# Attention over a ±4-channel window: the edge products of the band read 32 rows instead of 128 and run as a group of their own, in pairs on separate rows of TensorE

## The chip, the cores and the metric

The kernel runs on one NeuronCore of one Trainium2 chip. The metric is the device time of one execution in microseconds (us), the median of the runs shown; lower is better. TensorE (PE in the profile) has a clock of two levels, 1.2 and 2.4 GHz; the profile gives the granted clock as a share of 2.4 GHz, so 0.50 is the lower level.

## What is computed

One block of a MetaFormer on x of 128 images, 256 channels, 9 by 9 pixels (81 pixels, called HW), all in fp32: a layer norm over channels, a convolution-attention part that is added to x, then a mixture of 8 experts (2 for each token) that is added as well. The change sits in the first of the two attentions. Cut to what matters:

```
k1 = grouped 1-d conv of x along channels (9 taps, one kernel per pixel)
a  = softmax over 9 taps of W2 @ relu(bn(W1 @ [x, k1])) + b2     # a[b, d, c]: 9 weights per channel
v  = depthwise 3x3 conv of x + bias                              # v[b, c, h, w]
pad_v = v with 4 channels of zeros on either side
out1[b, c] = sum over d of pad_v[b, c + d] * a[b, d, c]  + k1    # a band of 9 channels around c
out2 = second, spatial attention
x1   = x + alpha * out1 + (1 - alpha) * out2
```

The sum over d is a product with a band matrix: for one image, a 256 by 256 matrix that is zero farther than 4 from its diagonal, times v of 256 channels by 81 pixels.

## The kernel before

The kernel is written engine by engine, with semaphores set by hand; nothing is reordered by a scheduler, so the order on each engine is the order of the code. The stages follow one another: the norm and k1; the two depthwise convolutions; the attention stage; routing of the tokens; the experts; gathering and output.

In the attention stage the images go in 32 groups of 4 (G = 4), and two groups make one turn of the loop (PAIRS = 16). For each group, PE does these steps, named as in the code:

- keys (line 514): the logits' first layer, 8 matmuls of 512 columns;
- band (lines 565 to 571): the band products of a group one or two steps older;
- spatial_1, tap_logits and spatial_2 (lines 524 and 526, 541, 533): the second attention's layers and the tap logits;
- unmasked (line 553): transposes that turn expanded tap weights into the band matrices of a group.

pe_turn writes the order out by hand: keys, band (odd group of the turn before), spatial_1, tap_logits, spatial_2, unmasked, then the same for the second group of the pair with the even group's band.

band splits the 256 channels in two halves of 128 rows, since PE takes 128 input rows and 128 output rows at a time. Four products are needed for an image. Two are full: output channels 0 to 127 from input channels 0 to 127 (a0_s, columns 0 to 127, into bank 6 of the accumulator ps), and output channels 128 to 255 from input channels 128 to 255 (a1_s, columns 32 to 159, into bank 7). Two are edges: the last output channels of the first half also need the first channels of the second half (a1_s, columns 0 to 31, into rows 96 to 127 of bank 6), and the first 4 output channels of the second half need the last channels of the first (a0_s, columns 128 to 131, into rows 0 to 3 of bank 7). Outside the band a0_s and a1_s hold zeros. Four images lie side by side in each bank, 81 columns each. `start=True` on a matmul makes it overwrite, `start=False` makes it add to what is there.

Around band: DVE makes a0_s and a1_s in mask_bands (lines 891 and 893, semaphore msk_c) and adds the result to x1 in add_band (line 918, which waits for band_p). GpSimd (POOL) waits for band_p too, before it loads v of a later group into vc_s (line 1463). SyncE (SP) loads the other inputs of a group when DVE has finished the group two before it. ACT does the activations. One fp32 matmul of the code shows in the trace as two pieces on PE, each with a weight load of its own (PEld).

Of the kernel before, what the change touches and what calls it, by code (L numbers as in the profile page):

```python
# [5 lines left out]
HW = H * W  # L6
# [7 lines left out]
G = 4  # L14
# [33 lines left out]
def metaformer_kernel(nc, x, taps, tap_bn, tap_rows, toeplitz_mask, ident, band_masks, rot_masks, zstrings,  # L48
# [14 lines left out]
    with ctx:  # L63
# [46 lines left out]
        def take(parts, *dims):  # L110
            n = 1
            for d in dims:
                n *= d
            a = pool_[0:parts, cursor[0]:cursor[0] + n]
            cursor[0] += n
            assert cursor[0] <= C * HW
            names = "abcde"[:len(dims)]
            if len(dims) > 1:
                a = a.rearrange(f"p ({' '.join(names)}) -> p {' '.join(names)}",
                                **{m: d for m, d in zip(names, dims)})  # L120
            return a
# [26 lines left out]
        ps = ctx.enter_context(nc.psum_tensor("ps", [128, 8, 512], fp32))  # L148
# [24 lines left out]
        xc_s, vc_s, kc_s, xr_s, kr_s = (take(128, 2, HALVES, G, HW) for _ in range(5))  # L173
# [7 lines left out]
        a0_s = take(128, G, BAND0)  # L181
        a1_s = take(128, G, BAND1)
# [236 lines left out]
        def _(pe):  # L419
# [48 lines left out]
            with pe.Fori(0, C // CHUNK) as i:  # L468
# [4 lines left out]
                for n in range(9):  # L473
# [4 lines left out]
                    for m in range(9):  # L478
                        last = nc.tensor.matmul(flat[:, m * 2 * CHUNK:(m + 1) * 2 * CHUNK].rearrange("p (v c) -> p v c", v=2),
                                                mask_s[:, n * 9 + m, :],  # L480
                                                tapc_s[:, :, :],
                                                start=True, stop=True)
                    last.then_inc(S["mb_p"], 1)
                for k in range(per_chunk):
                    q, par = i * per_chunk + k, k % 2
# [9 lines left out]
                    for c in range(QUAD):  # L495
                        o = ps[:, b0 + c // 2, (c % 2) * 2 * HW:(c % 2 + 1) * 2 * HW]
                        last = nc.tensor.matmul(o, pt_s[:, par, c, :], m_s[:, k * QUAD + c, :, :]  # L497
                                                .rearrange("p v n -> p (v n)"), start=True, stop=True)
# [4 lines left out]
            for h in range(HALVES):  # L503
                last = nc.tensor.matmul(ps[:, 6, 0:EXPERTS], ones_s[:, :], router_s[:, h, :], start=h == 0, stop=h == 1)
# [52 lines left out]
            def band(g, par, i):  # L557

                pe.wait_ge(S[f"v_in{par}"], 32 * i)
                pe.wait_ge(S["msk_c"], 2 * (g + 1) + CREDIT)  # L560
                pe.wait_ge(S["x1_c"], g + CREDIT)
                for b in range(G):
                    v0, v1 = vc_s[:, par, 0, b, :], vc_s[:, par, 1, b, :]
                    o = slice(b * HW, (b + 1) * HW)
                    nc.tensor.matmul(ps[:, 6, o], a0_s[:, b, 0:128], v0, start=True, stop=False,  # L565
                                     skip_group_check=True)
                    nc.tensor.matmul(ps[96:128, 6, o], a1_s[:, b, 0:32], v1, start=False, stop=True,  # L567
                                     skip_group_check=True)
                    nc.tensor.matmul(ps[:, 7, o], a1_s[:, b, 32:160], v1, start=True, stop=False,  # L569
                                     skip_group_check=True)  # L570
                    last = nc.tensor.matmul(ps[0:4, 7, o], a0_s[:, b, 128:132], v0, start=False, stop=True,  # L571
                                            skip_group_check=True)
                last.then_inc(S["band_p"], 1)

            def pe_turn(i, first=False, front=True, back=True, late=True):

                if front:
                    keys(2 * i, 0, i, first)
                if late:
                    band(2 * i - 3, 1, i - 1)  # L580
                if front:
                    spatial_1(2 * i, 0, i)
                    tap_logits(2 * i, 0)
                    spatial_2(2 * i)
                if back:
                    unmasked(2 * i - 2, 0, i)
                if front:
                    keys(2 * i + 1, 1, i)
                if back:
                    band(2 * i - 2, 0, i)  # L590
                if front:
                    spatial_1(2 * i + 1, 1, i)
                    tap_logits(2 * i + 1, 1)
                    spatial_2(2 * i + 1)
                if back:
                    unmasked(2 * i - 1, 1, i)
# [4 lines left out]
            with pe.Fori(2, PAIRS) as i:  # L601
                pe_turn(i)
            pe_turn(PAIRS, front=False)
            band(GROUPS - 1, 1, PAIRS)

# [985 lines left out]
```

## Time and profile before

| | |
|---|---|
| device time, median of 3 runs | 1827.84 us (1827.51 to 1829.89) |
| span of the one profiled execution | 1881.2 us (no other time is recorded for it) |
| PE busy, share of the span | 76% |
| DVE, ACT, POOL busy | 60%, 40%, 34% |
| attention stage in the profiled execution | about 384 to 875 us |

A share of the whole span is an average over stages with different limits; the rows further down are of the attention stage alone. PE's records are pipelined: two matmuls that follow each other overlap in their durations, so what one costs is read from the distance between the ends of two, as the chain view gives it. That chain is followed back from the last instruction: at each step to what released it, or to the instruction before it on its engine.

### The profile page before, as it was taken

The page shows a single profiled execution, that of the slowest core. Times are in us where ns is not written, and L with a number is a line of the kernel's source. Part 1 is how long each engine was busy: PE and PEld are TensorE (multiplying, and loading weights), DVE is VectorE, ACT ScalarE, POOL GpSimd, SP SyncE. Part 2 cuts the span into 40 slices and gives each one's busy share as a digit, 9 for nine tenths or more (in the row PEclk, how much of TensorE's full clock was granted, in tenths as well). Part 3 has the DMA queues.
Part 4 walks back from the last instruction along what each step waited for, and adds up shares of the span by engine and source line. Part 5 has one row for each costly group of instructions (what it writes and reads, how often), then busy time and mean ns, then how long its engine had stood idle before and what let it go on. Part 6 is the DMA issues. An engine that isn't in the chain of part 4 may idle for free.

```text
span 1881.2 us, 38992 instructions
## 1 busy us (share of the span) xinstructions
PE 1423.0 (76%) x9926; PEld 1155.6 (61%) x9927; DVE 1127.2 (60%) x3074; ACT 753.2 (40%) x1752; POOL 648.2 (34%) x561
## 2 busy tenths in 40 slices
PE   0485889879999999998454442899999999993222
PEld 0474888846666666666444442688888888882111
DVE  6893333346766766764677667466666666663333
ACT  0572444434444434433565553333333333332211
POOL 0350111123333334330555555255555455441000
PEclk9996788789999999995555555899999999996555
DMA  8434454377667667641333234223332333324999
GB/s 291 114 107 167 167 191 179 146 205 187 153 151 182 152 157 172 154 112 55 104 98 110 93 104 142 77 84 90 90 90 86 92 93 90 90 74 129 194 197 159
DMA packets 310870, 250.50 MB, mean 133 GB/s; under 512 B 184329, under 2 KB 289374, under 8 KB 310132
## 3 DMA queue, kind: packets, MB, share of 16 engines
q1 hardware_dynamic: 290527, 196.96, 40.4%
q0 software_dynamic: 20320, 53.28, 8.6%
q8 instruction: 9, 0.15, 0.0%
q14 instruction: 14, 0.11, 0.0%
HBM read 152.07 MB, written 105.57 MB: 137 GB/s over the span
## 4 chain that ended last, share of the span: by engine, by line
PE 65%; DVE 12%; DMA 8%; issue 6%; ACT 4%; SPq 3%; another core or an unknown queue 1%; DVEq 1%; ACTq 0%; POOLq 0%; POOL 0%
PE ps L690 13%; PE ps L675 12%; PE ps L514 6%; DMA aux<-y_d 4%; PE ps L497 4%; PE ps L463 4%; PE ps L541 3%; PE ps L569 3%; PE ps L565 2%; ACT pool_ L1267 2%; PE ps L524 2%; PE ps L659 2%; PE ps L533 2%; PE ps L567 2%; PE ps L526 2%
## 5 line engine op out<-in xcount | busy, mean ns | idle before, releaser
L1491 POOL DMA_INDIRECT y_d<-pool_,to_s x176 | 254.9, 1449 | 285.6 <-DVE pool_ L1184 249.4
L690 PE MATMUL ps<-pool_,aux 128*128 x2112 | 249.8, 274 | 5.2 <-DVE aux L1176 3.5
L675 PE MATMUL ps<-aux,pool_ 128*128 128x256 f16 x2112 | 247.4, 274 | 0.8 <-ACT aux L1391 0.6
L690 PEld LDWEIGHTS ps<-pool_,aux 128*128 128x128 f16 x2112 | 198.5, 98 | 50.8 <-issue 23.7
L675 PEld LDWEIGHTS ps<-aux,pool_ 128*128 x2112 | 207.0, 98 | 25.9 <-issue 1.4
L1471 POOL DMA_INDIRECT rows_d<-aux,idx_s x162 | 157.9, 975 | 159.3 <-issue 87.3
L1391 ACT ACTIVATE aux<-ps,b_s 128x256 f32<-128x256 f32 x352 | 138.4, 475 | 162.5 <-DVE aux L1176 162.1
L1184 DVE SCALAR_TENSOR_TENSOR pool_<-ps,pool_ 128x512 f32<-128x512 f32 x88 | 60.9, 692 | 140.2 <-PE ps L690 140.2
L1463 POOL DMA_DIRECT2D pool_<-v_d x64 | 50.1, 783 | 271.1 <-PE ps L571 269.8
L718 PE MATMUL ps<-ident_s,aux 128*128 128x128 f32 x162 | 41.6, 429 | 122.4 <-DVE aux L1216 122.4
L514 PE MATMUL ps<-pool_,se_w_s 81*81 81x512 f32 x256 | 118.7, 607 | 6.0 <-DMA pool_<-k_d 6.0
L1383 ACT ACTIVATE aux<-ps 128x512 f16<-128x512 f32 x88 | 52.5, 597 | 174.9 <-PE ps L659 174.9
L718 PEld LDWEIGHTS ps<-ident_s,aux 128*128 128x128 f32 x162 | 30.8, 221 | 133.0 <-DVE aux L1216 133.0
L1176 DVE TENSOR_TENSOR aux<-aux 128x1024 f16<-128x1024 f32 x88 | 107.8, 1225 | 3.1
L1302 ACT ACTIVATE pool_<-ps,sa_ab 128x324 f32<-128x324 f32 x64 | 39.7, 621 | 160.0 <-PE ps L526 160.0
L1447 POOL COPY aux<-big 128x324 f32 x64 | 29.3, 459 | 213.9 <-PE ps L463 184.7
L1216 DVE SCALAR_TENSOR_TENSOR aux<-aux,wt_s 128x256 f32<-128x256 f32 x81 | 34.5, 481 | 105.4 <-ACT aux L1409 103.6
L463 PE MATMUL ps<-ident_s,aux 128*81 128x128 f32 x512 | 76.8, 299 | 25.5 <-POOL aux L1447 25.5
L853 DVE COPY aux<-ps 81x512 f32<-81x512 f32 x64 | 43.9, 686 | 86.0 <-PE ps L463 86.0
L632 PE MATMUL ps<-aux,before_s 128*128 128x8 f32 x54 | 16.0, 370 | 103.9 <-DVE aux L1059 80.8
L1314 ACT ACTIVATE pool_<-ps,pool_ 128x81 f32<-128x81 f32 x256 | 79.7, 338 | 29.1 <-DVE pool_ L884 29.1
L497 PE MATMUL ps<-pool_,aux 82*128 82x162 f32 x512 | 90.0, 325 | 0.0
(203 smaller groups left out, 3160.9 us busy)
## 6 DMA issues: line engine op xcount, KB each, us to landing
pool_<-rows_d SPq DMA_DIRECT2D x88, 258.0 KB
aux<-y_d SPq DMA_DIRECT2D x54, 384.0 KB, 7.1
big<-in_x SPq DMA_DIRECT2D x2, 5184.0 KB, 21.0
xn_d<-big SPq DMA_DIRECT2D x16, 648.0 KB, 3.0
v_d<-aux SPq DMA_DIRECT2D x64, 162.0 KB, 2.0
ks_d<-aux SPq DMA_DIRECT2D x64, 162.0 KB, 2.0
pool_<-xn_d SPq DMA_DIRECT2D x32, 324.0 KB
pool_<-k_d SPq DMA_DIRECT2D x32, 324.0 KB
```

The costliest lines, as they stand in the source:

```text
L463: last = nc.tensor.matmul(ps[0:HW, 4 + par, c * BS:(c + 1) * BS], xq_s[:, par, c, :], ident_s[:, :], start=True, stop=True)
L497: last = nc.tensor.matmul(o, pt_s[:, par, c, :], m_s[:, k * QUAD + c, :, :] .rearrange("p v n -> p (v n)"), start=True, stop=True)
L514: last = nc.tensor.matmul(ps[0:HW, n, :], se_w1_s[:, k, :], kq_s[:, par, k, 2 * n:2 * n + 2, :].rearrange("p b j -> p (b j)"), start=k == ...
L675: last = nc.tensor.matmul(o, w_s[:, a, bass.ds(e * (4 * PIECE) + (k * HID + j * 128), 128)], xh_s[:, par, b, k * SLOTS:(k + 1) * SLOTS], s ...
L690: last = nc.tensor.matmul(ps[:, 6 + par, s * C:(s + 1) * C], hh_s[:, par, a, j, s * 128:(s + 1) * 128], w_s[:, b, bass.ds(e * (4 * PIECE) ...
L718: last = nc.tensor.transpose(ps[:, 2 * par + h, s * 128:(s + 1) * 128], mix_s[:, par, s, h * 128:(h + 1) * 128], ident_s[:, :])
L1176: nc.vector.tensor_tensor(lo, hf_s, hi, ALU.subtract).then_inc(S["hlo_c"], 1)
L1184: nc.vector.scalar_tensor_tensor(yo_s[:, par], ps[:, 6 + par, :].rearrange("p (s c) -> p s c", s=2), 1.0 / WSCALE, b2_s[:, bass.ds(e * C, ...
L1314: ins = nc.scalar.activation(e_s[:, par, h, b, :], ps[:, 2 + h, b * HW:(b + 1) * HW], ACT.Exp, bias=sm_s[:, par, 2, j:j + 1], accum_out=sm ...
L1391: nc.scalar.activation(hf_s[:, j * SLOTS:(j + 1) * SLOTS], ps[:, 2 + 2 * par + j // 2, (j % 2) * SLOTS:(j % 2 + 1) * SLOTS], ACT.Gelu, bia ...
L1471: nc.gpsimd.indirect_dma_start(out=rows_d[:, :], out_offset=bass.IndirectOffsetOnAxis(ap=idx_s[:, slot, k:k + 1], axis=0), in_=xf_s[:, slo ...
L1491: nc.gpsimd.indirect_dma_start(out=y_d[:, :], out_offset=bass.IndirectOffsetOnAxis(ap=to_s[:, par, k:k + 1], axis=0), in_=yo_s[:, par, k, ...
```

## The change

The full products of a group's four images come first, the edges after them in a loop of their own. An edge now names only the 32 input rows in which its band matrix is not zero: rows 0 to 31 of the second half for the one, rows 96 to 127 of the first half for the other. The products, their number and their columns are the same. Since all images of a group lie in one bank, only the first full product into each bank now has `start` set. The last edge signals band_p as before. No wait is added or removed.

```diff
                 for b in range(G):
                     v0, v1 = vc_s[:, par, 0, b, :], vc_s[:, par, 1, b, :]
                     o = slice(b * HW, (b + 1) * HW)
-                    nc.tensor.matmul(ps[:, 6, o], a0_s[:, b, 0:128], v0, start=True, stop=False,
+                    nc.tensor.matmul(ps[:, 6, o], a0_s[:, b, 0:128], v0, start=b == 0, stop=False,
                                      skip_group_check=True)
-                    nc.tensor.matmul(ps[96:128, 6, o], a1_s[:, b, 0:32], v1, start=False, stop=True,
+                    nc.tensor.matmul(ps[:, 7, o], a1_s[:, b, 32:160], v1, start=b == 0, stop=False,
                                      skip_group_check=True)
-                    nc.tensor.matmul(ps[:, 7, o], a1_s[:, b, 32:160], v1, start=True, stop=False,
+                for b in range(G):
+                    v0, v1 = vc_s[96:128, par, 0, b, :], vc_s[0:32, par, 1, b, :]
+                    o = slice(b * HW, (b + 1) * HW)
+                    nc.tensor.matmul(ps[96:128, 6, o], a1_s[0:32, b, 0:32], v1, start=False, stop=True,
                                      skip_group_check=True)
-                    last = nc.tensor.matmul(ps[0:4, 7, o], a0_s[:, b, 128:132], v0, start=False, stop=True,
+                    last = nc.tensor.matmul(ps[0:4, 7, o], a0_s[96:128, b, 128:132], v0, start=False, stop=True,
                                             skip_group_check=True)
                 last.then_inc(S["band_p"], 1)
```

Only PE's order changes, and only inside band. The first place is in the loop over the turns, where PE comes from keys (line 514) into band; a row is a line of the code, the operation, what it writes and reads, and the output's rows by columns. Before:

```order
L514 MATMUL ps<-pool_,se_w_s 81x512 x4
L559 ISA
L560 ISA
L561 REGISTER_ALU
L565 MATMUL ps<-pool_ 128x81
L567 MATMUL ps<-pool_ 32x81
L569 MATMUL ps<-pool_ 128x81
L571 MATMUL ps<-pool_ 4x81
```

The same place in the changed kernel, where line 565 is still the full product into bank 6 and line 567 is now the full product into bank 7:

```order
L514 MATMUL ps<-pool_,se_w_s 81x512 x4
L559 ISA
L560 ISA
L561 REGISTER_ALU
L565 MATMUL ps<-pool_ 128x81
L567 MATMUL ps<-pool_ 128x81
L565 MATMUL ps<-pool_ 128x81
L567 MATMUL ps<-pool_ 128x81
```

Each image had full, edge, full, edge; now the eight full products of a group stand together.

The second place is the end of the same band, before spatial_1 (line 524). Before:

```order
L569 MATMUL ps<-pool_ 128x81
L571 MATMUL ps<-pool_ 4x81
L521 REGISTER_ALU
L522 REGISTER_ALU
L524 MATMUL ps<-pool_,sa_w_s 128x324
```

After, with the edges at lines 572 (32 output rows) and 574 (4 output rows):

```order
L567 MATMUL ps<-pool_ 128x81
L572 MATMUL ps<-pool_ 32x81
L574 MATMUL ps<-pool_ 4x81
L572 MATMUL ps<-pool_ 32x81
L574 MATMUL ps<-pool_ 4x81
L572 MATMUL ps<-pool_ 32x81
L574 MATMUL ps<-pool_ 4x81
L572 MATMUL ps<-pool_ 32x81
L574 MATMUL ps<-pool_ 4x81
L521 REGISTER_ALU
L522 REGISTER_ALU
L524 MATMUL ps<-pool_,sa_w_s 128x324
```

The eight edges of the group now follow its last full product, the two kinds in turn.

## Rows read from the trace of the kernel before

**Rows 1.** The page: granted clock in 40 slices; the chain by engine.

```profile
PEclk9996788789999999995555555899999999996555
...
PE 65%; DVE 12%; DMA 8%; issue 6%; ACT 4%; SPq 3%; another core or an unknown queue 1%; DVEq 1%; ACTq 0%; POOLq 0%; POOL 0%
```

**Rows 2.** Stretches: start:end, us, busy by engine, granted clock, DMA share, GB/s.

```profile
427.20:835.00 407.80, 407.80 (x2164) 267.46 (x2163) 279.37 (x636) 173.72 (x592) 142.80 (x112) 1.00 0.67 161
840.00:854.30 14.30, 9.28 (x45) 6.01 (x43) 13.41 (x33) 4.71 (x18) 2.58 (x3) 0.69 0.10 23
854.34:862.65 8.31, 8.31 (x33) 5.15 (x34) 0.00 (x0) 0.00 (x0) 0.00 (x0) 0.50 0.00 1
```

**Rows 3.** The chain through one group: start us, us, engine, line, pieces.

```profile
639.35 3.43 PE ps L514 x8
642.78 0.18 PE ps L565 x2
642.97 0.26 PE ps L567 x2
643.23 0.38 PE ps L569 x2
643.61 0.23 PE ps L571 x2
643.84 0.38 PE ps L565 x2
...
647.59 0.74 PE ps L524 x2
648.33 0.55 PE ps L526 x2
...
652.84 0.87 PE ps L553 x8
653.72 3.44 PE ps L514 x8
```

**Rows 4.** Weight loads by shape, 452.58 to 826.12 us: busy us, mean ns, idle before.

```profile
L565 PEld LDWEIGHTS ps<-pool_ 128*128 128x128 f32 x208 | 33.1, 188 | 24.6 <-issue 13.4
...
L567 PEld LDWEIGHTS ps<-pool_ 128*32 128x32 f32 x208 | 14.3, 108 | 8.5
L571 PEld LDWEIGHTS ps<-pool_ 128*4 128x4 f32 x208 | 9.4, 84 | 8.5
```

**Rows 5.** The chain through the second last group's band and the transposes behind it.

```profile
854.34 0.69 PE ps L565 x2
855.03 0.41 PE ps L567 x2
855.44 0.65 PE ps L569 x2
856.09 0.36 PE ps L571 x2
...
862.65 1.90 PE ps L553 x8
```

**Rows 6.** DVE in order of time, one turn: start, us, instruction, idle before, releaser.

```profile
637.97 1.04 DVE L874 TENSOR_REDUCE pool_<-ps 128x4 f32<-128x324 f32 x2 [3.77 <-PE ps L533]
...
650.25 0.82 DVE L918 TENSOR_TENSOR big<-big,ps 128x648 f32 x1
652.34 1.04 DVE L874 TENSOR_REDUCE pool_<-ps 128x4 f32<-128x324 f32 x2 [1.27 <-PE ps L533]
...
655.11 0.48 DVE L893 TENSOR_TENSOR pool_<-ps,band_s 128x320 f32<-128x320 f32 x1
...
662.10 0.83 DVE L918 TENSOR_TENSOR big<-big,ps 128x648 f32 x1 [1.61 <-PE ps L571]
666.70 1.04 DVE L874 TENSOR_REDUCE pool_<-ps 128x4 f32<-128x324 f32 x2 [3.77 <-PE ps L533]
```

**Rows 7.** The chain's last long wait for a load in the attention stage.

```profile
416.77 6.81 DMA pool_<-k_d
```

## The prediction, made before the changed kernel ran

> **What bounds the kernel now.** I began with the page's row of the granted clock and its chain by engine: PE holds most of the chain, and the clock is at its upper level from the tenth slice to the eighteenth [rows 1]. A share of the whole span says nothing about band, so I cut out the stretch from the first band to the last one that runs at full pace. From 427.20 to 835.00 us PE is busy for all of 407.80 us, at a granted clock of 1.00 (2.4 GHz), while DVE is busy for 69% of it and the DMA engines for 67% [rows 2]. So PE's own stream of instructions is the limit there, and what it no longer has to do shortens the stage, as long as nobody else becomes the limit.
>
> Next I followed the chain through one group. It goes through PE's steps one after another without a wait; keys begin at 639.35 and again at 653.72, so a group costs 14.37 us [rows 3]. 28 such periods and one band (28 x 14.37 + 4.8 = 407 us) fill the stretch, which makes 29 bands in it. Of the other three, one runs beside DVE's chain after 840 us, and the last two run at 1.2 GHz: in the stretch of the second last one the granted clock is 0.50 [rows 2].
>
> **What a band costs, taken apart.** A band takes from 642.78 to 647.59 us, 4.81 us [rows 3]. Its first product shows 0.18 us, later full ones 0.38, the 32-row edge 0.26, the 4-row edge 0.23; 0.18 + 0.26 + 0.38 + 0.23 + 3 x (0.38 + 0.26 + 0.38 + 0.23) = 4.80.
>
> The streaming of columns: keys take 3.43 us for 8 pieces of 512 columns, 0.84 ns a column, so a piece of 81 columns streams for 0.068 us, and the two pieces of a product for 0.136. The weight loads: 128 columns show 188 ns, 32 show 108 and 4 show 84 [rows 4]. The 80 ns between the first two go with 96 columns, 0.83 ns each, so the columns take 0.107, 0.027 and 0.003 us.
>
> Now the 4-row edge: 0.23 - 0.136 - 0.003 leaves 0.091. The 32-row edge: 0.26 - 0.136 - 0.027 leaves 0.097. A full product behind an edge: two loads (the second covers the first stream) and one stream are 0.282, and 0.38 - 0.282 leaves 0.098. So about **0.095 us is lost wherever the shape of the product changes**, in which PE neither streams nor loads. Two rows bear it out. The first product of the band follows keys without a change of shape and costs 0.18 instead of 0.38. The 8 transposes of one shape cost 0.87 us, 0.109 a piece, which is the load of 128 columns alone: streams and gaps are hidden there [rows 3].
>
> **The change, step by step, at the full clock.**
>
> *The full products.* Sixteen pieces of one shape follow keys: 0.18 us for the first two as now, then 14 x 0.109 = 1.53. Sum 1.71 us.
>
> *Into the edges.* One change of shape, 0.095, and one exposed load, 0.027. Sum 0.12 us.
>
> *The edges.* Eight products, 16 pieces. No row of the trace shows two matmuls on different rows of the array, so I bound this from both sides. If each piece waits for the one before, they take 16 x 0.068 = 1.09 us. If a product runs beside its partner on the other rows, the pieces of one kind still follow each other, and the second kind is one piece behind: 9 x 0.068 = 0.61 us. A third, worse end: every step from one kind of edge to the other costs what a change of shape costs now; then the edges keep today's price, 4 x (0.26 + 0.23) = 1.96 us, and that includes the way in.
>
> The pairing has a rule behind it: the Trainium skill, "TensorE: Matmul & The Clock Gate", section "Part 3: Packing small matmuls — row/col tiling", says that matmuls on different 32-row strips start about 4 ns apart, in program order, while one matmul on 32 rows alone takes as long as on 128. By it the sum is the one with 0.61, and had the edges stayed unpaired, fewer rows would have saved nothing; the trace shows neither. On the third end the skill's "TensorEngine Tiling (Array Packing)", section "Key Properties", says that changing the tiling mode drains the engine and changing only the tile does not. The trace agrees on the first half, with the 0.095 us; by the second half the 1.96 would not come.
>
> *Out of the edges.* The way into spatial_1 is paid in its first product, 0.74 us against 0.55 for the next [rows 3], and stays.
>
> New band: 1.71 + 0.12 + 0.61 = 2.44 us, 2.37 less than 4.81. Over 29 bands: **68.7 us**.
>
> **The last two bands**, at 1.2 GHz. Now (0.69 or 0.65) + 0.41 + 0.65 + 0.36 for an image, 8.31 us for a group [rows 2, 5]. Eight transposes take 1.90 us, so sixteen full pieces 3.80; edges 9 x 0.135 = 1.22, the way in 0.14. Sum 5.16, 3.15 less; **6.3 us** for two. Both lie on the chain, which there runs from DVE's masks through band to add_band.
>
> **Who else must keep up.** A turn of two groups goes from 28.73 to 24.0 us. DVE first: from 637.97 to 651.07 us it works without a wait, 13.1 us, and then waits 1.27 for spatial_2 [rows 6]. With groups of 12.0 us it comes 1.1 us late to the second group of a turn. What is late next: its masks are done at 655.59, and PE comes to that band at about 657.15 (keys at 653.72 plus 3.44 [rows 3]); of these 1.56 us about 0.45 is left. Then it catches up: add_band there waited 1.61 us for band, and 3.77 us pass idle before the next turn [rows 6]. 28.73 less these three waits is 22.1 us, DVE's least for a turn, under 24.0. The DMA engines' 67% of 28.73 us become 80% of 24.0. The v loads of POOL and add_band hang on band_p, which comes earlier. Only at the start do loads end last, before keys at about 423.6 [rows 7]; groups right behind it may catch up with their loads again, and I charge 2 us (between 0 and 4), an estimate from that one wait of 6.81 us and the idle DMA share.
>
> **The sum.** 68.7 + 6.3 - 2 = 73 us. The profiled execution has a span of 1881.2 us, 53.4 over the median of the runs. Where it lost them I can't read; band's distances repeat to 0.01 us, so I carry 73 us over as it is: 1827.8 - 73 = **1755 us**, 4.0% less. Were the stage stretched by the same 2.8%, it would be 2 us less gain. If the way in and out of edges of 32 rows is shorter than today's, 0.04 us in two places of 29 bands give 2 us more. Its own range is 1748 to 1763.
>
> **The rivals.**
>
> *One after another.* The edges of a pair don't overlap: band 2.92 us, 29 x 1.89 = 55, plus 2 x 2.2 at the lower clock, less 1: **1769 us**. For it: the trace never shows two streams at once. Against: nor has it anything that could.
>
> *Every edge pays a change of shape.* Band 1.71 + 1.96 = 3.67, 29 x 1.14 = 33, plus 2.9: **1792 us**. For it: today each step between shapes pays, whichever way. Against: that the two kinds of edges now have the same rows and probably the same size.
>
> *Another engine takes over.* The masks come after PE is ready for band (the 0.45 us above), or a group's loads land late at 80% DMA. Each us of waiting in a turn costs 14 us in all; with one, 1769, with two, 1783. For it: the masks' margin shrinks from 1.56 to 0.45 us and the DMA engines' idle share from 33% to 20%. Against: DVE's 22.1 us.
>
> *The other side: the clock falls.* If TensorE dropped to 1.2 GHz within the stage, a group would take 2 x 9.56 + 5.16 = 24.3 us, 9.9 more than now. It decides from 29 x 2.37 / (9.9 + 2.37) = 5.6 groups on; all 29 would give about **2110 us**. For it: after the idle of 840 to 854 us the clock stays at 0.50 for 8.31 us though PE is busy throughout [rows 2]. Against: in 407.8 us of unbroken work it never fell, and the change leaves fewer gaps (2 for a band, not 16).
>
> *It does nothing.* Only if the unprofiled stage hangs on something the profiled one doesn't, among the 53.4 us: **1828 us**.
>
> **How the numbers follow.** Paired edges 0.52, one after another 0.18, another engine 0.11, every edge pays 0.10: faster 0.91. Nothing 0.03: same. Clock 0.06: slower. 0.2%, or 3.7 us, is about what a measurement of this kernel can tell from no change. The predicted time is that of paired edges. The range goes from 1745 (a few us more than reckoned at the way in and out, no wait at the start) to 1795, which takes in the serial case, the waits and the change of shape at every edge; what it leaves out is the last two cases and some of the edges of the others, under 2 in 10.
>
> **What would show it.** In the chain after, a group of about 12.0 us with: full products at 0.22 us each (0.109 a piece) and no 0.38; the first edge about 0.12 above its stream; edges of a pair in 0.14 us together (paired), 0.27 (one after another) or 0.49 (a change of shape at each). DVE's wait before the second reduction of a turn gone, and PE without a wait at line 565. Granted clock 1.00 throughout. Wrong would be: PE waiting for DVE's masks or for loads in most turns, or a clock below 1.00.

## The result, and the profile after

The changed kernel takes **1765.85 us** (median of 4 runs, 1765.32 to 1772.31) against 1827.67 us for the kernel before beside it (4 runs, 1823.94 to 1829.89): a ratio of 0.9665, 95% interval 0.9642 to 0.9689. The time fell by 61.8 us, where 73 were predicted. One run further down, of the kernel that holds POOL back from the second turn on, fell in a slower state (1867.5 us) and is left out of that kernel's time and ratio. The profiled execution of the changed kernel has a span of 1763.8 us. Behind line 574 its line numbers are 3 higher than before; full products are now lines 565 and 567, edges 572 and 574, DVE's masks 894 and 896.

The page's row of the granted clock, which answers to [rows 1]: the upper level again lasts from the tenth slice to the eighteenth, but a slice is now 44.1 us long, and was 47.0.

```profile
PEclk9995878879999999995555558999999999995555
```

The windows view of the stretch in which bands run at full pace, and of one of two short stretches inside it (columns as in [rows 2]):

```profile
440.00:775.00 335.00, 325.53 (x2037) 229.38 (x2037) 275.12 (x599) 163.17 (x550) 139.35 (x108) 0.99 0.78 184
...
677.40:680.80 3.40, 3.40 (x21) 2.36 (x16) 3.13 (x4) 0.20 (x2) 1.67 (x3) 0.50 0.79 215
```

PE was busy for all of its stretch before [rows 2]. Now it is idle for 9.5 us of 335, at a clock of 0.99, while DVE went from 69% to 82%: DVE is almost the limit too. The second row is one of two dips of the clock to its lower level, 3.4 us each (677.4 and 779.8 us).

The chain through a band that waits for nobody, then one that waits, then the second last one at the lower clock (start, us, what), which answers to [rows 3, 5]:

```profile
621.54 3.44 PE ps L514 x8
624.98 0.18 PE ps L565 x2
625.16 0.22 PE ps L567 x2
...
626.73 0.16 PE ps L572
626.89 0.07 PE ps L574
...
627.40 0.74 PE ps L524 x2
...
649.52 0.41 DVE pool_ L896
649.98 0.45 PE ps L565 x2
...
801.33 0.69 PE ps L565 x2
...
805.01 0.23 PE ps L572
...
806.23 1.90 PE ps L553 x8
```

The first band takes from 624.98 to 627.40, **2.42 us**; 2.44 was predicted, and it was 4.81 [rows 3]. Full products cost 0.22 us instead of 0.38, all eight edges 0.67 us together. The second one comes by way of DVE's mask at line 896, and its first product is dearer by 0.27 us, because its load lies open. The third takes 4.90 us (5.16 predicted, 8.31 before).

PE in order of time, the edges of a group (start, us, line, out<-in, rows*columns, pieces, idle before). Durations overlap; the starts tell:

```profile
649.98 0.45 PE L565 MATMUL ps<-pool_ 128*128 128x81 f32 x2 [1.02 <-DVE pool_ L896]
...
651.92 0.25 PE L572 MATMUL ps<-pool_ 32*32 32x81 f32 x1
651.92 0.30 PE L574 MATMUL ps<-pool_ 32*4 32x81 f32 x2
652.01 0.23 PE L572 MATMUL ps<-pool_ 32*32 32x81 f32 x1
652.07 0.23 PE L574 MATMUL ps<-pool_ 32*4 32x81 f32 x1
```

Each kind starts a piece about every 0.07 us, which is the 0.068 us that 81 columns stream, and both kinds do so at once: the edges run in pairs.

PE's waits from 400 to 800 us (engine, line, releaser: us in total, times, longest):

```profile
PE ps L565 <- DVE pool_ L896: 8.2, 8, 1.0
...
PE ps L514 <- DMA pool_<-k_d: 2.2, 4, 0.7
```

In eight turns PE waits 1.02 us for the masks of the band in the turn's second half, which it never did before. What made DVE late is in its order of time, first two groups that follow each other on DVE, then POOL:

```profile
641.68 1.66 DVE L909 TENSOR_TENSOR pool_<-pool_ 128x648 f32<-128x648 f32 x1
643.38 0.83 DVE L911 TENSOR_TENSOR pool_<-pool_ 128x648 f32<-128x648 f32 x1
644.44 1.88 DVE L913 SCALAR_TENSOR_TENSOR big<-pool_,alpha_s 128x648 f32 x1 [0.23 <-DVE pool_ L911]
...
651.99 0.83 DVE L909 TENSOR_TENSOR pool_<-pool_ 128x648 f32<-128x648 f32 x1
...
653.92 0.89 DVE L913 SCALAR_TENSOR_TENSOR big<-pool_,alpha_s 128x648 f32 x1 [0.23 <-DVE pool_ L911]
...
641.84 1.92 POOL L1459 TENSOR_SCALAR pool_<-pool_,alpha_s 128x648 f32<-128x648 f32 x1
643.95 1.68 POOL L1462 TENSOR_TENSOR pool_<-pool_ 128x648 f32<-128x648 f32 x1 [0.18 <-POOL pool_ L1459]
```

The same two instructions take 1.66 and 1.88 us in the first group and 0.83 and 0.89 in the second. In the first, POOL multiplies and adds (lines 1459, 1462: alpha times k1, plus x) at the same time. That is 1.8 us more on DVE, and of the masks' margin, which the prediction put at 0.45 us, nothing is left. These are the eight turns with a wait. In six others POOL's multiply meets line 911 instead, which then takes 1.32 to 1.71 us (1.46 at 593.74 us, for one), and PE does not wait for the masks.

**The account.** The attention stage went from 384.0–873.8 us to 383.6–814.0, 59.4 us less. Bands gave 29 x 2.39 = 69.3 and the last two 6.8. So 16.7 us went elsewhere, and the rows name 16.0: mask waits 8.2 with 8 x 0.27 of weight loads laid open, 2.2 of waits for keys' inputs, and 2 x 1.7 from the two dips.

### The profile page after: what moved, and what is told of

Its sections match the earlier page's. It is cut to its first block, busy times and chain, and to the rows that moved or that the text cites. A ratio compares the mean times of both kernels' runs of the same rounds, so it can differ in the third digit from the quotient of the medians.

```text
span 1763.8 us, 38992 instructions
## 1 busy us (share of the span) xinstructions
PE 1348.7 (76%) x9926; PEld 1129.9 (64%) x9927; DVE 1137.5 (64%) x3074; ACT 752.9 (43%) x1752; POOL 648.6 (37%) x561
## 4 chain that ended last, share of the span: by engine, by line
PE 53%; DVE 20%; DMA 11%; issue 7%; ACT 4%; SPq 3%; DVEq 1%; ACTq 0%; POOLq 0%; POOL 0%
PE ps L693 14%; PE ps L678 13%; DMA aux<-y_d 5%; PE ps L497 5%; PE ps L463 4%; ACT pool_ L1270 2%; PE ps L514 2%; PE ps L662 2%; DMA pool_<-k_d 2%; PE ps L479 2%; PE ps L541 2%; DVE pool_ L763 1%; PE ps L524 1%; DMA aux<-u_d 1%; PE ps L533 1%
## 5 line engine op out<-in xcount | busy, mean ns | idle before, releaser
L1412 ACT ACTIVATE aux<-aux,wt_s 128x256 f32<-128x256 f32 x81 | 35.2, 497 | 130.3 <-DMA aux<-y_d 130.3
L463 PEld LDWEIGHTS ps<-ident_s,aux 128*81 128x81 f32 x512 | 69.0, 170 | 25.6 <-POOL aux L1450 25.6
## 6 DMA issues: line engine op xcount, KB each, us to landing
aux<-y_d SPq DMA_DIRECT2D x54, 384.0 KB, 6.7
```

Of the source, the lines that this page charges most:

```text
L463: last = nc.tensor.matmul(ps[0:HW, 4 + par, c * BS:(c + 1) * BS], xq_s[:, par, c, :], ident_s[:, :], start=True, stop=True)
```

## The experiments

Two things were to be settled: whether POOL's arithmetic beside DVE is what took the missing 11 us, and what it is about the new edges that saves time: 32 rows, the grouping, or separate rows of PE.

**POOL's arithmetic out of DVE's way.** In the changed kernel, POOL's multiply waits until DVE has finished line 913 of the group before:

```diff
                     pool.wait_ge(S[f"rk_in{par}"], 64 * (i + 1))
+                    pool.wait_ge(S["t_c"], g + CREDIT)
                     settle()
```

> The changed kernel, and POOL starts its multiply and add for a group (lines 1459 and 1462) only when DVE has finished the group before it, so that they no longer run while DVE works through lines 908 to 913. Theory A (PE's wait for the masks comes from these collisions, which double two DVE instructions in every second group): lines 909 and 913 stay at 0.84 and 0.89 us throughout, PE's wait at line 565 in the steady stretch goes, a turn takes 24.0 us instead of 25.1 on average, time 1750 to 1756 us. Theory B (DVE is full at this pace, or the loads come late, whatever POOL does): 1764 to 1768 us, the wait stays.

Measured: 1751.0 us, ratio 0.9606 (0.9582 to 0.9630). DVE's costliest lines from 440 to 775 us, grouped by line (count | busy us, mean ns | idle before), of the changed kernel:

```profile
L913 DVE SCALAR_TENSOR_TENSOR big<-pool_,alpha_s 128x648 f32 (+1 forms) x27 | 32.0, 1185 | 6.0 <-DVE pool_ L911 6.0
...
L909 DVE TENSOR_TENSOR pool_<-pool_ 128x648 f32<-128x648 f32 x27 | 29.2, 1080 | 0.9
```

and of this experiment:

```profile
L913 DVE SCALAR_TENSOR_TENSOR big<-pool_,alpha_s 128x648 f32 (+1 forms) x27 | 24.1, 893 | 6.0 <-DVE pool_ L911 6.0
...
L909 DVE TENSOR_TENSOR pool_<-pool_ 128x648 f32<-128x648 f32 x28 | 23.3, 833 | 1.0
```

with its window over the same stretch:

```profile
440.00:775.00 335.00, 334.95 (x2122) 238.50 (x2122) 266.62 (x629) 172.07 (x588) 140.48 (x112) 1.00 0.82 192
```

The doubled instructions are gone, PE is busy throughout, the clock stays at 1.00, and a turn takes the predicted 24.0 us instead of 25.1 on average. The wait has a price in the first turn, where nothing is in its way: the first band is done at 439.2 us instead of 429.2. Only part of that is the wait itself. PE there waits 2.3 us for ACT ahead of line 524, and then the granted clock is 0.50 from 420.0 to 433.7 us. Five of the six profiles with POOL's wait in the first turn have such a fall, of 10 to 14 us, between 400 us and their first band, and no profile without it has one. The sixth (output rows shared, below) begins its first band at 431.1 us, against 426.5 in the changed kernel and 436.5 here: by these single profiles, about half of the price is the wait, and half the clock.

The same wait in the kernel before (no band edit):

> The kernel before with the same later start of POOL alone. Theory A: PE is the limit there and nothing collides, so within 4 us of the kernel before (1824 to 1832). If the later start were worth something by itself, whatever the band costs, it would show here: 1815 us or less.

Measured: 1821.41 us, ratio 0.9995 (0.9979 to 1.0010). Nothing: in the kernel before, the lines of DVE that answer to 909, 911 and 913 show 0.83 and 0.89 us in every group from 424 to 840 us anyway. The collision itself came only with the faster bands.

POOL's arithmetic left out of the changed kernel altogether (alpha x k1 + x is then missing from x1):

```diff
                     pool.wait_ge(S[f"rk_in{par}"], 64 * (i + 1))
-                    settle()
-                    nc.gpsimd.tensor_scalar(kr_s[:, par], kr_s[:, par], alpha_s[:, 0:1], None, ALU.mult).then_inc(S["ch_g"], 1)
-                    pool.wait_ge(S["ch_g"], g + 1)
-                    settle()
-                    nc.gpsimd.tensor_tensor(kr_s[:, par], kr_s[:, par], xr_s[:, par], ALU.add).then_inc(S["r1_c"], 1)
+                    pool.sem_inc(S["r1_c"], 1)
```

> The changed kernel without POOL's multiply and add (lines 1459 and 1462): alpha times k1 plus x is left out of x1. POOL's v loads keep their times. Theory A (the collisions with DVE make the wait for the masks): lines 909 and 913 of DVE at 0.84 and 0.89 us throughout, PE's wait at line 565 gone, turn 24.0 us, 1749 to 1756 us if the kernel before takes 1822. Rival (the later v loads and not the arithmetic gave POOL's later start its gain): as the changed kernel, 1760 to 1766 us.

Measured: 1740.53 us, ratio 0.9546 (0.9525 to 0.9566); turns of 24.0 us, lines 909 and 913 at 0.83 and 0.89, no wait for masks in the running turns. That is faster than either range. In the running turns it equals the wait; the rest is the start of the stage, where the clock does not fall (first band done at 428.7).

So the wait was put only where it is needed, for the first group of a turn, from the second turn on (against the first experiment):

```diff
-            with pool.Fori(0, PAIRS) as i:
+            def residual_and_load(i, late):
...
-                    pool.wait_ge(S["t_c"], g + CREDIT)
+                    if late and par == 0:
+                        pool.wait_ge(S["t_c"], g + CREDIT)
...
+            residual_and_load(0, False)
+            with pool.Fori(1, PAIRS) as i:
+                residual_and_load(i, True)
```

> The changed kernel with POOL's later start only where the collisions are: for the first group of a turn, and not in the first turn, so that the stage's start is as in the changed kernel. Theory A: turns of 24.0 us as with the later start everywhere, and the band of the first groups some 5 to 10 us earlier; ratio to the kernel before 0.952 to 0.957 (about 1740 us if that takes 1824). Rival (the later start is needed in every group, or the first turn is not what the general one loses): 0.958 to 0.961.

Measured: **1743.45 us** (median of five runs), ratio 0.9573 (0.9559 to 0.9587), a hair above what was expected, and the lowest ratio here of a kernel that leaves nothing out. Turns of 24.0 us, first band done at 427.1, and no fall of the clock ahead of it.

**Is it the 32 rows?** The order of before, edges on 32 rows:

```diff
-                    nc.tensor.matmul(ps[96:128, 6, o], a1_s[:, b, 0:32], v1, start=False, stop=True,
+                    nc.tensor.matmul(ps[96:128, 6, o], a1_s[0:32, b, 0:32], v1[0:32], start=False, stop=True,
...
-                    last = nc.tensor.matmul(ps[0:4, 7, o], a0_s[:, b, 128:132], v0, start=False, stop=True,
+                    last = nc.tensor.matmul(ps[0:4, 7, o], a0_s[96:128, b, 128:132], v0[96:128], start=False, stop=True,
```

> The kernel before with the edges on 32 rows, in their old places between the full products. If the grouping carries the saving: still a change of shape at every product, band 4.6 to 4.8 us, 1820 to 1828 us. If fewer rows carry it (a change of shape costs less from 32 rows, or an edge's stream runs beside a full product): band 4.2 us or less, 1808 us or less.

Measured: 1872.13 us, ratio 1.0272 (1.0245 to 1.0298): slower, a miss. Its chain through the middle of one band:

```profile
642.54 0.25 PE ps L567 x2
642.80 0.38 PE ps L569 x2
643.18 0.23 PE ps L571 x2
...
645.41 0.65 PE ps L569 x2
646.05 0.36 PE ps L571 x2
```

and its window:

```profile
440.00:820.00 380.00, 380.00 (x1784) 244.37 (x1784) 230.84 (x536) 146.59 (x502) 118.01 (x93) 0.87 0.60 143
```

At the upper clock each product costs what it did on 128 rows (0.38, 0.25, 0.38, 0.23): a change of shape is as dear with 32 rows. But within the band the clock falls to 1.2 GHz, though PE is busy in every one of the 380 us: 0.87 over the stretch, and 13% of 380 us is 49, which is the loss of 50. With one kind of edge alone on 32 rows (the second pair of lines of that diff):

> The kernel before, with only the 4-row edge (line 571) on 32 input rows and all in its old place. Both kinds on 32 rows in place took 1872 us at a granted clock of 0.87 in the stage, though PE never waited. Theory A (fewer rows in use at the same pace bring the clock down): in between, clock below 1.00 in the stretch of the bands, 1830 to 1860 us. Theory B (only the first kind, or the change between two row restrictions, does it): clock 1.00 and the time of the kernel before within 4 us.

Measured: 1840.24 us, ratio 1.0092 (1.0072 to 1.0112). Its window:

```profile
440.00:820.00 380.00, 380.00 (x1930) 248.12 (x1929) 248.79 (x573) 156.22 (x528) 130.72 (x102) 0.95 0.64 155
```

Again PE without a gap, and a clock in between (5% of 380 us is 19; lost are 18). In the kernel before, the whole of its full-paced stretch has 1.00 [rows 2].

The other half alone, the new order with edges on all 128 rows:

```diff
-                    v0, v1 = vc_s[96:128, par, 0, b, :], vc_s[0:32, par, 1, b, :]
+                    v0, v1 = vc_s[:, par, 0, b, :], vc_s[:, par, 1, b, :]
...
-                    nc.tensor.matmul(ps[96:128, 6, o], a1_s[0:32, b, 0:32], v1, start=False, stop=True,
+                    nc.tensor.matmul(ps[96:128, 6, o], a1_s[:, b, 0:32], v1, start=False, stop=True,
...
-                    last = nc.tensor.matmul(ps[0:4, 7, o], a0_s[96:128, b, 128:132], v0, start=False, stop=True,
+                    last = nc.tensor.matmul(ps[0:4, 7, o], a0_s[:, b, 128:132], v0, start=False, stop=True,
```

> The changed kernel with the edges on all 128 rows as before, grouped behind the full products, so that no two edges can run side by side. Band 1.71 + 0.12 + 1.09 = 2.9 us against 2.4 in the changed kernel. Theory A (DVE and not PE sets the pace of a turn there): the half us is mostly swallowed, 1766 to 1771 us. If PE still set the pace: 0.5 x 29 + 2 = 16 us more than the changed kernel, 1780 to 1784 us.

Measured: 1759.2 us, ratio 0.9665 (0.9638 to 0.9691), the changed kernel's own ratio. The reason that had been given for it was wrong, as PE in order of time shows:

```profile
658.51 0.26 PE L572 MATMUL ps<-pool_ 128*32 128x81 f32 x1
658.52 0.30 PE L574 MATMUL ps<-pool_ 128*4 128x81 f32 x2
658.61 0.23 PE L572 MATMUL ps<-pool_ 128*32 128x81 f32 x1
```

Edges that read all 128 rows pair just as well: a start every 0.07 us for each kind. PE also waits for masks (10.3 us in ten waits of 1.02 or 1.03), with the same doubled lines on DVE. So the rows don't matter for what the edges cost in the grouped order, and the pairing needs something else. In one thing this kernel differs from the changed one: its clock never falls behind these waits, as its window shows:

```profile
440.00:775.00 335.00, 323.66 (x2029) 227.26 (x2029) 277.17 (x605) 164.86 (x567) 134.51 (x107) 1.00 0.79 185
```

**What the pairing needs.** Four kernels with POOL's wait of the first experiment, so that PE alone sets the pace: edges with input rows apart or shared, output rows apart or shared. Rows and output rows apart is the first experiment itself. Input rows shared (the diff just shown, on top of the wait):

> The changed kernel with POOL's later start, so that PE is the limit again and what a band costs shows in the time, and with the edges on all 128 input rows: the two kinds share input rows and keep their separate output rows (96 to 127, and 0 to 3). Theory A (separate output rows are enough for two edges to run side by side; the restriction to 32 input rows brings nothing): edges 0.6 us a group, turn 24.0 us, within 4 us of the changed kernel with POOL's later start, 1747 to 1755 us if the kernel before takes 1822. Theory B (separate input rows are what lets them run side by side): the edges take 1.09 us, a turn 25.0, some 15 us more.

Measured: 1748.47 us, ratio 0.9587 (0.9567 to 0.9608). Output rows shared: the second edge is one of 32 columns into rows 96 to 127 of bank 7, from rows 96 to 127 (the 4 outputs' own edge is then left out):

```diff
-                    last = nc.tensor.matmul(ps[0:4, 7, o], a0_s[96:128, b, 128:132], v0, start=False, stop=True,
+                    last = nc.tensor.matmul(ps[96:128, 7, o], a0_s[96:128, b, 100:132], v0, start=False, stop=True,
```

> The changed kernel with POOL's later start; the second kind of edge is replaced by a product on input rows 96 to 127 that adds into rows 96 to 127 of bank 7 (32 columns of weights), so that the two kinds have separate input rows but the same output rows. The true 4-row edge is left out. Theory A: no pairing without separate output rows, edges 1.09 us, turn 25.0 us, 14 to 17 us more than with POOL's later start alone (about 1766 if the kernel before takes 1822). Theory B (separate input rows are enough): 1749 to 1755 us.

Measured: 1748.9 us, ratio 0.9589 (0.9567 to 0.9612). Both shared (the 4 outputs' own edge left out here too):

```diff
-                    last = nc.tensor.matmul(ps[0:4, 7, o], a0_s[96:128, b, 128:132], v0, start=False, stop=True,
+                    last = nc.tensor.matmul(ps[96:128, 7, o], a1_s[0:32, b, 0:32], v1, start=False, stop=True,
```

> As the one with separate input rows and the same output rows, but the second kind also reads rows 0 to 31: nothing is separate but the bank. The true 4-row edge is left out. Both theories: one after another, edges 1.09 us, turn 25.0 us, about 1766 if the kernel before takes 1822. This is the price without pairing, against which the other three are read.

Measured: 1766.99 us, ratio 0.9694 (0.9671 to 0.9718). The chain of the edges with output rows shared:

```profile
649.47 0.18 PE ps L572
649.65 0.01 PE ps L574
649.66 0.06 PE ps L572
...
650.15 0.74 PE ps L524 x2
```

and with both shared:

```profile
649.58 0.25 PE ps L572 x2
649.83 0.14 PE ps L574 x2
...
650.82 0.74 PE ps L524 x2
```

0.68 us for eight edges in the one, 1.24 in the other, in which each product takes the 0.14 us of its two streams. Either input rows apart or output rows apart is enough; with neither, edges run one after another. That explains 18 us between the last two kernels: 0.56 x 29 = 16, and 1.1 twice at half the clock. In the two profiles, the way from the first band's start to the last band's is 16.1 us longer with both shared; besides, that kernel's first band comes 3.2 us later, after a fall of the clock that the other does not have. The step from one kind to the other costs nothing beside, even there.

**How far ahead PE looks.** The four edges of one kind first, then those of the other (on top of the wait; line 577 is the second kind here):

```diff
+                for b in range(G):
+                    v0 = vc_s[96:128, par, 0, b, :]
+                    o = slice(b * HW, (b + 1) * HW)
                     last = nc.tensor.matmul(ps[0:4, 7, o], a0_s[96:128, b, 128:132], v0, start=False, stop=True,
```

> The changed kernel with POOL's later start, the edges not in turn but four of the first kind and then four of the second. Theory A (PE starts an edge of the other kind ahead of its place in the program, but only a little ahead): pairs form only around the change from one kind to the other, edges 0.9 to 1.09 us, turn 24.7 to 25.1, ratio 0.966 to 0.970. Theory B (it looks far enough ahead): as in turn, 0.957 to 0.961.

Measured: 1758.2 us, ratio 0.9656 (0.9636 to 0.9677), turns of 24.6 us, just under the expected 24.7. Its chain of edges:

```profile
655.65 0.47 PE ps L572 x5
656.12 0.01 PE ps L577
656.13 0.07 PE ps L572
...
656.34 0.29 PE ps L577 x5
656.62 0.74 PE ps L524 x2
```

Three of the second kind's eight pieces run beside the last ones of the first kind, although these are ahead of them in the program. So PE looks a little ahead, but not far: the pairs have to be written as pairs.

## Why the prediction was right or wrong

- **The number:** 1765.85 us lies in the stated range, but outside 1748 to 1763, the range of paired edges alone from which 1755 came. By the time alone, serial edges (1769) or one us of waiting in each turn (1769) would have fitted better; only the chain tells them apart. Of its own signs of being wrong two came: PE waited for masks in eight turns and for loads in four, of about fourteen, and the clock fell below 1.00 twice.
- **What bounds the kernel:** right. PE's own stream set the pace, and what band lost came out of the stage but for the 16.7 us of the account.
- **A loss of 0.095 us at a change of shape:** right. Without the changes full products cost 0.22 us; with 32 rows in place every one of them stayed. That the price doesn't hang on the rows was assumed and is now shown.
- **The edges:** right in size (0.67 us for edges and way in, against 0.73), incomplete in reason. "The partners here share no input rows, no output rows and no bank": any one of the first two is enough. The rows, by which the change is named, give nothing in the new order, as 128 rows take the same time. The serial rival's price, 1.24 us against 0.67, stands in the kernel with both shared.
- **The last two bands:** 6.8 us against 6.3.
- **Who else must keep up: the step that failed.** What failed is DVE's least for a turn, 22.1 us: it was read from a turn [rows 6] in which POOL's arithmetic didn't lengthen the lines 906 and 910 of before (a mean of 832 and 894 ns in that trace), and it was carried over as it was. In the new rhythm they meet in eight turns, DVE needs 1.8 us more there, and the margin of 0.45 us before the masks is gone. This is the rival "another engine takes over", at one wait in half the turns. It has been shown both ways: with POOL held back or idle, turns take 24.0 us. The Trainium skill, "SBUF — State Buffer", section "Who interferes with whom", says that a VectorE instruction with two inputs in SBUF contends with a GpSimd instruction that reads SBUF. The trace agrees for lines 909 (0.83 to 1.66 us) and 913 (0.89 to 1.88), while line 911 kept its 0.83 us at 643.38 us though POOL's add began during it, and took 1.46 us at 593.74 beside POOL's multiply.
- **Loads at the start:** 2 us were charged, and keys waited 2.2 us for their inputs. That the numbers agree is luck: the four waits lie in the running turns (before 460.06, 535.26, 609.33 and 736.93 us) and not at the start. They belong to the rival with late loads, at 0.5 us in four turns, and in the first experiment they are gone as well.
- **The clock:** "in 407.8 us of unbroken work it never fell" held for unbroken work in the new order, but not among full products with edges on 32 rows (0.95 and 0.87). In the changed kernel it fell twice, each time 2.2 us behind a mask wait of 1.02 or 1.03 us; six such waits brought no fall. With POOL held back the stretch from 440 to 775 us stays at 1.00, though the first turn does not. The waits and the doubled DVE lines together do not suffice: with edges on 128 rows, eleven such waits up to 783 us brought no fall. That points to the edges on 32 rows, but with one profile of each it is not shown.
- **The unread 53.4 us of the profile before:** they lay behind the attention stage. From the stage's end at 873.8 us to SyncE's load of the experts' rows (line 367, at 1178.76) routing took 305 us there, and 251 in the profile after (814.0 to 1064.80); why is open. Carrying the gain over unchanged was right.

With the collision out of the way the kernel gains 78 us (ratio 0.9573): the sum of 73, the 2 that it charged for loads (no such wait is left in that trace) and 0.5 more in the last two bands; the 2 that remain are inside the interval, which is 5 us wide.

## What to carry to other kernels

Write products of one shape next to each other, and put small ones in pairs that differ in their input rows or in their output rows; cutting rows alone gains nothing, and among full products it can cost the clock. When the bounding engine gets faster, look at which instructions of two other engines will newly run at the same time, not only at how long each took before. And if a rhythm brings a collision, hold back the one with time to spare, but not in the first turn, if it stands on the chain there.

## What the runs showed of the hardware

- Matmuls overlap when they differ in input rows or in output rows (0.68 us for eight products of 81 columns against 1.24 with neither), with 32 or 128 rows alike.
- Such matmuls start out of the program's order: in the changed kernel the second kind of edge starts its first piece at 651.92 us, ahead of the second piece of the first kind (652.01), and with the kinds apart three pieces of the second kind run among the first kind's last ones. The Trainium skill, "TensorE: Matmul & The Clock Gate", section "Part 3: Packing small matmuls — row/col tiling", says that they start in program order. Here the trace differs, and it decides.
- A busy PE doesn't keep the clock. With PE busy in every one of 380 us the granted clock was 1.00 with all edges on 128 rows, 0.95 with one kind on 32, and 0.87 with both, all of them among full products. Behind the full products, both kinds on 32 rows kept it at 1.00 from 440 to 775 us as long as PE did not wait (the first experiment).
- One POOL instruction over 648 fp32 columns lengthens a DVE instruction with two inputs in SBUF from 0.83 to 1.66 us and from 0.89 to 1.88 (lines 909 and 913), but not in all cases of an overlap (line 911: 0.83 us at 643.38, 1.46 at 593.74).
